# TensorE signals at drain instructions and GpSimd waits less often in the two gather passes of a two-layer graph network

## What is computed

```
# layer 0: a maximum over the edges of each destination
msgs = z[edge_dst] @ Wd + z[edge_src] @ Ws + edge_weight[:, None] * ww[None, :] + bm
agg  = segment_max(msgs, edge_dst);  hidden = relu(z @ W1a + agg @ W1b + b1);  z0 = hidden @ W2 + b2
x = layernorm(x + z0)
# layer 1: two softmaxes over the edges of each destination
h = x @ node_fc_W + b;  hs, hd = h[src], h[dst];  a = sum(hs * hd)
g = sigmoid(relu(he @ rel_att_W1 + b1) @ rel_att_W2 + b2)        # he: edge features through a layer
alpha, beta = seg_softmax(a, dst), seg_softmax(g, dst)
h_att = segment_sum(alpha * (hs @ node_att_W));  h_rel = segment_sum(beta * (hs @ rel_att_W))
x = layernorm(x + gate * where(deg > 0, relu([h_att, h_rel] @ out_fc_W + b), h) + (1 - gate) * x)
```

## Time and profile before

| | us |
|---|---|
| median of 3 runs | 2765.78 (2756.91 to 2768.17) |
| the profiled execution | 2743.96 |
| its span, first to last instruction | 2742.2 |
| pass 1, first gather to last gather | 41.6 to 1206.8 |
| pass 2, first gather to last gather | 1347.4 to 2617.9 |
| mean granted TensorE clock | 0.808 of 2.4 GHz |

### The profile page before, as it was taken

How to read it: one execution, slowest core, us unless ns; L and a number is a source line. 1 busy time by engine, 2 the same in 40 slices (tenths; PEclk the granted TensorE clock), 3 DMA queues, 4 the chain that set the end, 5 groups by cost and what they waited for, 6 DMA issues and landing times. The chain is left out here.

```text
span 2742.2 us, 43228 instructions
## 1 busy us (share of the span) xinstructions
PE 1835.3 (67%) x9891; PEld 1131.7 (41%) x9891; DVE 1333.0 (49%) x5220; ACT 1117.0 (41%) x3305; POOL 1648.3 (60%) x1705
## 2 busy tenths in 40 slices
PE   3577776776767676554656776767667666666675
PEld 3222222221222222113445665656556565565565
DVE  3555555554434344324634544445445544554459
ACT  1233333333333333332444544444444444444448
POOL 3766666666767677646455655556565565655625
PEclk8798888888889798786867777777877777877788
DMA  8433333333333233322411211211222121211213
GB/s 226 167 116 125 106 118 108 118 106 123 108 105 121 87 122 108 114 87 73 129 43 48 52 50 50 53 47 54 52 50 50 52 50 52 52 49 52 54 42 114
DMA packets 115984, 235.04 MB, mean 86 GB/s; under 512 B 32910, under 2 KB 68231, under 8 KB 106423
## 3 DMA queue, kind: packets, MB, share of 16 engines
q0 software_dynamic: 52832, 109.39, 16.2%
q1 hardware_dynamic: 56522, 97.21, 9.6%
q10 hardware_dynamic: 6540, 27.42, 2.9%
HBM read 166.01 MB, written 67.89 MB: 85 GB/s over the span
## 5 line engine op out<-in xcount | busy, mean ns | idle before, releaser
L462 POOL DMA_INDIRECT d_region<-d_h,d_region x784 | 750.2, 957 | 549.7 <-issue 241.4
L209 POOL DMA_INDIRECT acc<-d_src_product,b_region x784 | 785.0, 1001 | 381.5 <-issue 204.6
L642 PE MATMUL banks<-acc,b_region 64*128 64x512 f32 x1176 | 340.5, 685 | 274.0 <-ACT gate_col L747 130.1
L850 DVE SCALAR_TENSOR_TENSOR acc<-b_region,acc 128x128 f32<-128x128 f32 x784 | 271.2, 346 | 364.8 <-DMA acc<-d_src_product,b_region 343.7
L1570 DVE TENSOR_TENSOR acc<-acc,banks 128x160 f32 x784 | 252.6, 322 | 346.1 <-remote 148.0
L1369 PE MATMUL banks<-d_region 128*128 128x128 f32 x1568 | 303.7, 353 | 11.6 <-issue 11.6
L642 PEld LDWEIGHTS banks<-acc,b_region 64*128 64x128 f32 x1176 | 104.9, 202 | 469.3 <-issue 180.2
L1372 PE MATMUL banks<-d_region,pick 128*128 128x128 f32 x1568 | 288.9, 341 | 11.8 <-issue 11.7
L1372 PEld LDWEIGHTS banks<-d_region,pick 128*128 128x128 f32 x1568 | 271.4, 257 | 14.7 <-issue 14.7
L1369 PEld LDWEIGHTS banks<-d_region 128*128 128x128 f32 x1568 | 268.9, 257 | 18.3 <-issue 12.8
L861 DVE SCALAR_TENSOR_TENSOR acc<-acc,b_region 128x128 f32<-128x128 f32 x784 | 270.1, 345 | 9.5 <-remote 5.7
(11 more groups left out here) (261 smaller groups left out, 2439.0 us busy)
## 6 DMA issues: line engine op xcount, KB each, us to landing
d_runs<-acc SPq DMA_DIRECT2D x48, 1024.0 KB
acc<-ea ACTq DMA_DIRECT2D x25, 1024.0 KB
acc<-d_src_product,b_region POOLq DMA_INDIRECT x784
d_region<-d_h,d_region POOLq DMA_INDIRECT x784
d_region<-d_rel SPq DMA_DIRECT2D x49, 256.0 KB
hT<-xT SPq DMA_DIRECT2D x7, 448.0 KB, 7.0
d_src_product<-acc SPq DMA_DIRECT2D x7, 448.0 KB, 3.1
d_gates<-acc ACTq DMA_DIRECT2D x196, 6.0 KB
```

The costliest lines, as they stand in the source:

```text
L209: pool.indirect_dma_start(self.rows[:, s, j, :], None, d["B"], bass.IndirectOffsetOnAxis(self.idx[:, k:k + 1], 0)).then_inc(self.gathered[ ...
L462: pool.indirect_dma_start(rows[:, s, :], None, table, bass.IndirectOffsetOnAxis(idx[:, s:s + 1], 0)).then_inc(gathered[q], 16)
L642: last = nc.tensor.matmul(bank[4 + n % 2 * 2 + h][:, :], wf[h * DE:(h + 1) * DE, m * P:(m + 1) * P], ea[h * DE:(h + 1) * DE, u % (2 * UC), ...
L850: nc.vector.scalar_tensor_tensor(rows[:, s, j, :], wwb, wgt[:, k:k + 1], rows[:, s, j, :], ALU.mult, ALU.add).then_inc(ch, 1)
```

## The change

Of TensorE's signals, seven move from the last matmul of a step to a drain instruction right behind it: `tm` and `dt` in pass 1, and all five of pass 2. A drain holds TensorE's own stream until what was issued before it has ended; the signal is then given by the drain. The small jobs of pass 1 keep their signals at matmuls, `sel` of `owner_rows` among them. On GpSimd, both waits for `tm` in pass 1 go. The leash to `dt` stays at the same four units, counted in groups now (LEASH = 8), and is asked in every group rather than every second. In pass 2 the wait for `weights_turned` goes, and LAG becomes 4.

```
-def gather_rows(nc, pool, t, table, idx, rows, idx_ready, rows_used, rows_turned, weights_turned, gathered, after_first):
+def gather_rows(nc, pool, t, table, idx, rows, idx_ready, rows_used, rows_turned, gathered, after_first):
...
             pool.wait_ge(rows_turned, it * NG + (NG + q - LAG + 1 + NG))
             pool.wait_ge(idx_ready, it * NG + (NG + q + 1))
             pool.wait_ge(rows_used, it * NG + (NG + q + 1))
-            gathers(q, range(0, GJ // 2))
-            pool.wait_ge(weights_turned, it * NG + (NG + q - LAGW + 1 + NG))
-            gathers(q, range(GJ // 2, GJ))
+            gathers(q)
...
-LAG = 3
-LAGW = 6
+LAG = 4
...
-LEASH = 4
-LOOKS_FROM = 12
+LEASH = 8
...
-                u = g // 2
+                if g >= LEASH + 2:
+                    pool.wait_ge(dt, (g - LEASH) // 2)
                 for j in range(GJ):
-                    if u > LEASH and (g % 2, j) == (0, 0):
-                        pool.wait_ge(dt, u - LEASH)
-                    if u >= LOOKS_FROM and (g % 2, j) == (0, 3):
-                        pool.wait_ge(tm, M * u - 4)
-                    if u >= LOOKS_FROM and (g % 2, j) == (1, 2):
-                        pool.wait_ge(tm, M * u - 3)
                     runs.gather(pool, d, g, j)
...
-                    last.then_inc(tm, 1)
+                    pe.drain().then_inc(tm, 1)
...
-                last.then_inc(dt, 1)
+                pe.drain().then_inc(dt, 1)
...
-                last.then_inc(tp, 1)
+                pe.drain().then_inc(tp, 1)
```

More of the change, by code:

```diff
@@ L451, in iterations_but_one, with gathers @@
     return eng.value_load(t["nit"][0:1, 1:2], min_val=MINIT - 1, max_val=MAXIT - 1)
-def gather_rows(nc, pool, t, table, idx, rows, idx_ready, rows_used, rows_turned, weights_turned, gathered, after_first):
+def gather_rows(nc, pool, t, table, idx, rows, idx_ready, rows_used, rows_turned, gathered, after_first):
     rest = iterations_but_one(pool, t)
-    def gathers(q, part=range(GJ)):
+    def gathers(q):
         hold(pool)
-        for j in part:
+        for j in range(GJ):
             s = q * GJ + j
@@ L1355, in spread @@
                 nc.tensor.matmul(BOUNDS[:, 0:8], vals[q % 2][:, 8:9].to_broadcast([P, P]), sel[q % 2][:, 0:8],
-                                 start=True, stop=True).then_inc(vv, 1)
+                                 start=True, stop=True)
+                pe.drain().then_inc(vv, 1)
             def turn_weights(it, q):
@@ L1371, in sums @@
                 for k in range(1 + M):
-                    last = nc.tensor.matmul(Z[q % 2], pick[:, M - k:M - k + P], wts[q % 2][:, :, k, :],
+                    nc.tensor.matmul(Z[q % 2], pick[:, M - k:M - k + P], wts[q % 2][:, :, k, :],
                                             start=(k == 0), stop=(k == M))
-                last.then_inc(ug, 1)
+                pe.drain().then_inc(ug, 1)
             def group(it, q, end):
```

11 lines of the change are left out of this document (6 added, 5 removed).

## The result

The changed kernel takes 3148.21 us, the median of 4 runs (3120.78 to 3156.19), beside 2765.31 us for the kernel before (4 runs): a ratio of 1.137, 95% interval 1.130 to 1.145. It is slower by 383 us where 2380 us was forecast; the time also lies above the range (2320 to 2920). The profiled run took 3152.24 us with a span of 3150.3 us.

What follows compares the result with a forecast made beforehand. GpSimd's gathers were the nearest floor, kept from it by TensorE signals held during gathers; -124 us in pass 1 and -262 in pass 2 took 2744 to 2358 us, plus 22 for the runs' median: 2380 us, range 2320 to 2920.

Steps and rivals of the forecast that it cites:

- What bounds the kernel now: Both gather passes: TensorE's matmul signals are held while GpSimd gathers, its stops free them; 2437 of 2742 us.
- The floor: GpSimd's own gathering: 5.2 us a group in pass 1, 5.0 in pass 2, against 5.9 and 6.5 run.
- A drain's signal is not held: Both passes: drain signals escape the holding, GpSimd's stops go; 142 us less in pass 1, 282 in pass 2, before allowances.
- rival 2: Both passes: drain signals are held too, with TensorE standing behind them; 3020 us, 2870 to 3300, chance 0.14.
- The price of a drain: TensorE loses 0.35 us per drain, 0.23 to 0.5; pass 2's group takes 4.8 us, hidden under GpSimd's 5.0.
- The clock: TensorE in pass 2 runs mostly at 2.4 GHz, granted clock above 0.9; 20 us allowed for the rest.
- Rival 3: Drains work but TensorE stays at 1.2 GHz; pass 2 at 7.5 us a group, 3050 us, chance 0.08.
- GpSimd's fewer waits at nothing: Both passes: dropping the `tm` waits and loosening the `rows_turned` wait to LAG 4 gains nothing by itself.
- What was to show it: Trace signs: gathers 1.25 to 1.3 us apart if right; others for a wrong floor, rivals 1 or 2, drain price or clock.
- the last sentence: Pass 2: TensorE without foreign gaps and GpSimd waiting for `ug` mean a drain over 0.4 us or a low clock.

Runs made afterwards that it cites:

- i1: Kernel before with a measuring phase ahead: links signalled at matmul or drain while GpSimd rests, gathers or sets memory; chip 15, one execution, 3107.25 us.
- e1: Pass 1 as in the changed kernel, pass 2 as in the kernel before; chip 14, 2279.64 us, 1.000 of the kernel before.
- e3: GpSimd's waits as in the changed kernel, every TensorE signal at its matmul as before; chip 14, 2280.2 us, 1.000 of the kernel before.
- e2: Pass 1 as in the kernel before, pass 2 as in the changed kernel; chip 14, 2370.45 us, 1.039 of the kernel before.
- h4: GpSimd's waits as in the changed kernel, all signals at matmuls as before; chip 15, 2780.13 us, 1.014 of the kernel before.
- f1: The changed kernel again, unaltered, on chip 13; 3091.85 us, 1.129 of the kernel before.
- j1: Kernel before with a measuring phase ahead: signals at matmuls, 28 gathers per stretch, straight on or with memsets or halts between; chip 11, one execution, 3099.54 us.
- e5: Changed kernel with a second, signal-less drain ahead of each of pass 2's five; chip 13, 3163.76 us, 1.151 of the kernel before.
- g4: Changed kernel with one product of `Z` per group of pass 2 instead of four; chip 9, 2389.14 us, 1.049 of the kernel before.
- g1: All drains of the changed kernel, GpSimd's waits as in the kernel before; chip 9, 2368.47 us, 1.040 of the kernel before.
- g2: Changed kernel with `sel` of pass 1 at a drain too; chip 9, 2330.38 us, 1.022 of the kernel before.

## Why the prediction failed, step by step

- **What bounds the kernel now**: right in the main. Signals of TensorE are held while GpSimd gathers; i1 shows it alone, and chips without it run the kernel before at 2280 us. The floor was right in size: 5.2 us per group of pass 1 and 5.1 of pass 2 in e1 and e3, forecast as 5.2 and 5.0. The change doesn't lead there; another chip does. Wrong was that it takes a stop of GpSimd to free a signal: in i1 most of the late ones come while it gathers.
- **A drain's signal is not held**: this step failed, and the forecast with it. Pass 1 was to fall by 124 us and pass 2 by 262; they grew by 202 and 192. The step was given 0.60, and rival 2 (the signal held too, TensorE standing behind it, 3020 us, 2870 to 3300) 0.14. Rival 2 is what happened in pass 1: L633 stands 366 us, and the pass is 202 us longer. i1 has held drains of 2.24 to 13.71 us. The trace of before couldn't show it, as it has no drain beside gathers; the range should have carried rival 2 whole. It ended at 2920 inside of it. Rival 2's own range doesn't follow from its terms either: 130 us for pass 2 and 40 to 700 for pass 1 on 2766 are 2936 to 3596.
- **The price of a drain**: taken as 0.35 us from 0.23 to 0.5; measured 0.40 us (e2). The size was nearly right, the conclusion not: 3.06 + 5 x 0.35 = 4.8 us was read as hidden under GpSimd's 5.0 with 0.2 us to spare. With 0.40 the spare is gone at the full clock, and what the low stretches of the clock add is then seen: +86 us on a chip with nothing held. In pass 1 four drains in 10 us of unit cost nothing there (e1), as said.
- **The clock**: it was forecast to be mostly at 2.4 GHz, and 20 us were allowed. This is the most mis-sized term of pass 2. Windows of pass 2, of the kernel before, and under it of e2, to be read beside that of the changed kernel above (x of POOL counts the gathers, four a group):

```profile
1400.00:2600.00 1200.00, 830.59 (x5772) 714.38 (x5772) 591.12 (x2649) 563.52 (x2418) 708.75 (x741) 0.77 0.20 51
```

```profile
1200.00:2200.00 1000.00, 752.96 (x5659) 580.00 (x5658) 581.14 (x2605) 579.40 (x2378) 698.18 (x732) 0.92 0.25 60
```

| per group of pass 2 | TensorE busy | idle | sum | clock |
|---|---|---|---|---|
| before (185 groups) | 4.48 us | 1.99 us | 6.48 us | 0.77 |
| changed (174 groups) | 5.52 us | 1.95 us | 7.47 us | 0.70 |
| e2, the changed pass 2 on chip 14 (183 groups) | 4.11 us | 1.35 us | 5.46 us | 0.92 |

Idle time is of another kind now and no larger: 1.35 us as in e2, and 0.6 us more. Those 0.6 are standing only in part: a few drains of `tp` and `sT` are long (10.8 and 5.8 us the longest, in the records above), and the other gaps are somewhat longer than e2's. What grew is busy time. Beside e2 the same instructions take 5.52 us at 0.70 and 4.11 us at 0.92, so 1.4 us of the group go with the lower clock, 275 us in 196 groups. Beside the kernel before it is 1.04 us, with the clock down from 0.77 to 0.70; how much of that is the clock, and how much the overlap of steps that a drain ends, isn't separated. Rival 3 (TensorE at 1.2 GHz becomes the bound of pass 2, 7.5 us per group) named this and was given 0.08; the clock didn't stay low all the time, as it supposed.
- **GpSimd's fewer waits at nothing**: right on chips without held signals (e3, g3), and 39 us too little on the one that h4 ran on.
- **What was to show it**: the last sentence named the sign, no gaps of TensorE but its own and GpSimd waiting for `ug`, and gave drain price and clock as its causes. Both belong to it; the third, a drain that is held, wasn't on that list for pass 2, where its part is the smaller one.

The outcome is rival 2 in pass 1 and mostly rival 3 in pass 2, near 200 us each. Each rival priced both passes by its own cause alone, and no case had both causes. That 3148 us lies in rival 2's range is in part luck: its 7.2 us for a group of pass 2 came from 2.4 us of holding, and the 7.5 us measured have at most 0.6 of it. What stays open: why three chips hold and two don't, and how far the lower clock on those that hold (0.70 in the changed kernel and 0.74 in f1, 0.91 in e2, on the same code of pass 2) is the chip's own, or follows from the 0.6 us of further idle time. The shares of the two passes are read from the traces; neither pass was changed alone on a chip that holds.

## What to carry to other kernels

A drain doesn't avoid a late completion, it waits for it, and puts the engine itself in the queue behind. Before moving a signal to a drain, measure one link with the suspected neighbour at work: the phase of 24 links in i1 told in one run what the whole kernels before it had left open. If signals are late beside a long unbroken row of indirect transfers, a short piece of other work in the row is worth a try: it helped in j1's measuring phase, and no whole kernel has tried it. And repeat a surprising baseline on a second chip before explaining it.

## What the runs showed of the hardware

- While GpSimd issues indirect transfers without a break, TensorE's completions are held, after some 10 us and for 2 to 14 us at a time, with the signal at the matmul and at a drain (i1 on chip 15, j1 on chip 11 for the matmul; the kernels on chip 13 have the same gaps). On chips 9 and 14 the kernels show nothing of it; the measuring phase didn't run there. A row of memsets of 11.6 us held nothing, and in j1 a memset of 0.49 us between gathers prevented it, at the low level of the clock.
- A drain of TensorE behind each of five steps costs 0.40 us of the group apiece at the full clock (e2); a second one right behind it 0.07 us (e5), the clock's part included.
- Less work can be slower: with three of four products of `Z` left out the granted clock of pass 2 is 0.73 instead of 0.94 (g4, g1), and the kernel took 59 us longer than with them (g4, g2).
